# Shared pairs' halves by VectorE, other granules for masks, loads back and norms, and another order of the ring's slots

## Time and profile before

| | before |
|---|---|
| median of three runs | 2344.86 us |
| the profiled execution's own time | 2346.39 us |
| its span, first to last instruction | 2344.4 us |
| TensorE busy | 2286.9 us, 98% |
| VectorE, ScalarE, GpSimd busy | 1303.6, 748.2, 957.5 us |
| mean granted TensorE clock | 0.991 |
| DMA queues' share | 78% |
| landing of a plain weight (512 KB) | 4.4 us median |
| landing of a mixed weight (256 KB) | 3.2 us (ring), 3.6 us (extra slots) median |

### The profile page before, as it was taken

The page is one execution under the profiler, slowest core; times in us unless marked ns, Lnnn a source line. Parts: engine busy times, 40 slices in busy tenths (PEclk is TensorE's granted clock), DMA queues, the critical chain, the costliest instruction groups (busy, mean ns, idle before and its releaser), DMA issues.

```text
span 2344.4 us, 27397 instructions
## 1 busy us (share of the span) xinstructions
PE 2286.9 (98%) x10264; PEld 1891.1 (81%) x10264; DVE 1303.6 (56%) x1696; ACT 748.2 (32%) x1173; POOL 957.5 (41%) x686
## 2 busy tenths in 40 slices
PE   8999999999999999999999999898999999999899
PEld 7888787788888888888888888786788888877777
DVE  4332666857344448738235448687823545858660
ACT  3233554233343335202124326413113433632210
POOL 5455555587354522142034450516204544053610
PEclk9999999999999999999999999999999999999999
DMA  7799999878888878886678886666667887666755
GB/s 266 269 393 375 350 344 333 326 273 304 298 291 272 278 293 289 303 333 234 233 246 269 281 291 226 209 207 243 243 219 260 282 272 281 227 218 205 270 186 179
DMA packets 229158, 637.07 MB, mean 272 GB/s; under 512 B 23712, under 2 KB 32928, under 8 KB 225952
## 3 DMA queue, kind: packets, MB, share of 16 engines
q1 hardware_dynamic: 229024, 635.30, 78.0%
HBM read 483.10 MB, written 152.11 MB: 271 GB/s over the span
## 4 chain that ended last, share of the span: by engine, by line
PE 80%; DVE 10%; DMA 5%; issue 2%; SPq 1%; ACT 1%; POOL 1%; DVEq 0%; ACTq 0%
PE bank L1333 26%; PE bank L1335 26%; PE bank L1334 26%; PE bank L1353 1%; DVE acc L1627 1%; DMA mixed_w<-mixes 1%; DMA prod<-spilled_u 1%; DMA split_w<-w 1%; DVE prod L1908 1%; DMA w_more<-mixed_w 1%; DVE w L1973 1%; SPq L779 1%; DVE below L1806 1%; POOL w L1066 1%; DVE largest L1809 1%
## 5 line engine op out<-in xcount | busy, mean ns | idle before, releaser
L1066 POOL TENSOR_TENSOR w<-raw,w 128x512 fp32r<-128x512 f32 (+1 forms) x196 | 281.3, 1442 | 207.7 <-ACT w L1112 207.4
L1333 PE MATMUL bank<-w,prod_t 128*128 128x512 f32 x672 | 271.5, 404 | 10.5 <-DVE prod_t L2042 10.5
L1071 POOL TENSOR_TENSOR w<-w 128x512 fp32r<-128x512 f32 x138 | 196.2, 1446 | 207.6 <-ACT w L1287 207.3
L1335 PE MATMUL bank<-w,prod_t 128*128 128x512 f32 x672 | 264.7, 394 | 0.0
L1334 PE MATMUL bank<-w,prod_t 128*128 128x512 f32 x672 | 263.8, 393 | 0.0
L1333 PE MATMUL bank<-w,tok 128*128 128x512 f32 (+1 forms) x664 | 253.5, 382 | 3.9 <-POOL w L1066 3.0
L1335 PE MATMUL bank<-w,tok 128*128 128x512 f32 (+1 forms) x664 | 252.5, 380 | 0.0
L1334 PE MATMUL bank<-w,tok 128*128 128x512 f32 (+1 forms) x664 | 252.4, 380 | 0.0
L1333 PE MATMUL bank<-tok,w 128*128 128x512 f32 x640 | 249.0, 389 | 0.0
L1334 PE MATMUL bank<-tok,w 128*128 128x512 f32 x640 | 249.0, 389 | 0.0
L1335 PE MATMUL bank<-tok,w 128*128 128x512 f32 x640 | 249.0, 389 | 0.0
(11 more groups left out here) (219 smaller groups left out, 4681.4 us busy)
## 6 DMA issues: line engine op xcount, KB each, us to landing
w<-split_w SPq DMA_DIRECT2D x448, 512.0 KB, 4.4
split_w<-w SPq DMA_DIRECT2D x184, 512.0 KB, 6.2
w<-mixed_w SPq DMA_DIRECT2D x184, 256.0 KB, 3.2
w_more<-split_w SPq DMA_DIRECT2D x88, 512.0 KB, 5.2
w_more<-mixed_w SPq DMA_DIRECT2D x120, 256.0 KB, 3.6
rows<-x_dram SPq DMA_DIRECT2D x32, 512.0 KB, 5.3
mixed_w<-own SPq DMA_DIRECT2D x12, 1024.0 KB, 5.2
spilled_u<-prod SPq DMA_DIRECT2D x12, 1024.0 KB, 8.2
```

What stands on the lines that cost most here:

```text
L1066: pool.tensor_tensor(lo, words, hi, ALU.subtract).then_inc(lo_ready, 1)
L1071: pool.tensor_tensor(slot_of(g)[:, 1, :], slot_of(g)[:, 1, :].bitcast(F32), slot_of(g)[:, 0, :], ALU.subtract).then_inc(pool_lo, 1)
L1333: pe.matmul(out, left[0], right[0], start=first, stop=False)
L1335: return pe.matmul(out, left[1], right[0], start=False, stop=last)
```

## The change

- Pairs 5 and 6: VectorE lowers A12 (behind each k's sums) and A22 in `make_units`, and S1, S2, S4 in a new function `lower_sums`, right behind it. GpSimd keeps A11 and S3 (`lower_early`), with a semaphore of its own, and lowers T4's weights too, which VectorE did.
- In pairs 5 and 6 the extra slots take granules 4 to 7 of ten instead of 6 to 9.
- Wide blocks: the scratch of the picks lies over unit slots 2 to 4 (A12's and A22's words). Tiles 0 and 1 are picked at granules 175 and 177, tiles 2 and 3 at 209 and 210, and the choice is at 212 (before: 209, 211, 213, 215 and 218). ScalarE's cut of an odd hidden step waits for the picks that lie before it. The first two groups are masked at 213 and 214 (219, 220), and GpSimd multiplies their six chunks at 215 to 220 (221 to 226).
- Wide blocks: loads back of groups 0 to 3 at the last granules of products 2 to 5 of pair 6: 235, 239, 243, 247 (before 239, 251, 253, 255). Masks of groups 0 to 3 at 251, 253, 255, 257 (251, 255, 258, 261). Norms at 261, 264, 267, 270 (258, 261, 264, 267), the next block's first tokens at 275 and 277 (272, 273), their loads at 270 and 273 (266, 267).
- Block 0: ScalarE's counts three and four granules after VectorE's step instead of one and two. The own sets ten granules apart from 42 on (nine, from 44), mixed seven granules after the first load instead of five; the norm's constants at 164 instead of 158.

```diff
                     self.late_hi_at[odd + 9] = n
-                    self.units_lo_at.update({begun + 5: (n, "early"), odd + 8: (n, "A12"), odd + 10: (n, "A22"),
-                                             odd + 12: (n, "S1"), odd + 15: (n, "S2"), odd + 19: (n, "S4")})
+                    self.lower_at[odd + 2] = n
+                    self.units_lo_at[begun + 5] = n
...
         self.search_at = {m: k for k, m in enumerate(steps_at[1:COUNTS + 1])}
-        self.pick_from = self.start[("hidden", 2)] + 1 if wide else steps_at[COUNTS + 1]
-        self.search_end = self.pick_from + (2 if wide else 3) * TILES + 1
-        self.pick_at = {self.pick_from + (2 if wide else 3) * t: t for t in range(TILES)}
+        self.pick_from = steps_at[COUNTS + 1]
+        self.search_end = self.pick_from + 3 * TILES + 1
+        self.pick_at = {self.pick_from + 3 * t: t for t in range(TILES)}
+        if wide:
+            self.pick_from, begun = (self.start[("hidden", i)] + 3 - i for i in (1, 2))
+            self.pick_at = {self.pick_from + 1: 0, self.pick_from + 3: 1, begun: 2, begun + 1: 3}
+            self.search_end = begun + 3
         if wide:
-            self.back_at = {end["fast", SHARED_PAIRS[1], 3]: [0], shared_end: [1], out0 + 1: [2], out0 + 3: [3]}
-            read = {("up", c): out0 + at - 1 for c, at in enumerate((-1, 3, 6, 9))}
+            self.back_at = {end["fast", SHARED_PAIRS[1], q]: [c] for c, q in enumerate((2, 3, 4, 5))}
+            read = {("up", c): out0 + at - 1 for c, at in enumerate((-1, 1, 3, 5))}
...
                         for i, g in enumerate(GROUPS[:-1])}
-        self.mask_at[out0 + 9 if wide else out0 + 5 if later else out0 + 3] = GROUPS[-1]
+        self.mask_at[out0 + 5 if later else out0 + 3] = GROUPS[-1]
...
             self.read_hidden_at, self.hidden_at = {}, {}
-        self.norm_at = [out0 + 6 + (3 if later else 5) * t for t in range(TILES)]
-        self.tokens_at = [out0 + 20, out0 + 21] if later else [out1 + 2, out1 + 4]
+        self.norm_at = [out0 + (9 if wide else 6) + (3 if later else 5) * t for t in range(TILES)]
+        self.tokens_at = [out1 + 1, out1 + 3] if wide else [out0 + 20, out0 + 21] if later else [out1 + 2, out1 + 4]
         self.residual_load = [ups + 2, ups + 3, self.norm_at[0] + 3, self.norm_at[1] + 3]
-        self.tokens_load = [out0 + 14, out0 + 15] if later else [self.norm_at[2] + 3, self.norm_at[3] + 3]
+        self.tokens_load = [out0 + 18, out0 + 21] if wide else [out0 + 14, out0 + 15] if later else [self.norm_at[2] + 3, self.norm_at[3] + 3]
...
 SQUARE_LAG = 2
-COUNT_LAG = 1
+COUNT_LAG = [3, 1, 1, 1]
...
         _from, PHASE[_b, _phase[0]] = _m, _m
-        _order = [(_next + i) % RING for i in range(RING)] + list(range(RING, RING + EXTRA))
+        _order = [(_next + i) % RING for i in range(RING)]
+        _place = HALF if _phase[0] in SHARED_PAIRS else RING
+        _order[_place:_place] = range(RING, RING + EXTRA)
...
 OWN_SETS = range(FIRST_MIXES, FIRST_MIXES + 3 * HALF)
-OWN_FROM = {n: 44 + 9 * i for i, n in enumerate(OWN_SETS)}
+OWN_FROM = {n: 42 + 10 * i for i, n in enumerate(OWN_SETS)}
 OWN_LOADS = {at + i: (n, i) for n, at in OWN_FROM.items() for i in range(4)}
-OWN_AT = {at + 5: n for n, at in OWN_FROM.items()}
-OWN_STORES = {at + 6: n for n, at in OWN_FROM.items()}
-FIRST_NORM_LOAD = 158
+OWN_AT = {at + 7: n for n, at in OWN_FROM.items()}
+OWN_STORES = {at + 8: n for n, at in OWN_FROM.items()}
+FIRST_NORM_LOAD = 164
...
     _, p, q = granule.key
-    return products(p)[q] == VECTOR_LO and (p < SPILLED[0] or p in SHARED_PAIRS)
+    return products(p)[q] == VECTOR_LO and p < SPILLED[0]
...
-    return len(UNIT_LOS) * shared_round(b, n) + UNIT_LOS.index(what) + 1
+    names = EARLY_LOS if what in EARLY_LOS else UNIT_LOS
+    return len(names) * shared_round(b, n) + names.index(what) + 1
...
         below = sb("below", [P, GK, P], F32)
+        below_of = [over("below_wide", [P, GK, P], F32, u_at + 2 * HALF * 2 * P * 4) if wide else below for wide in WIDE]
+        assert GK * P <= 3 * HALF * 2 * P
...
-            def lower_units(b, n, what):
...
+            def lower_early(b, n):
...
                     if m in plan.units_lo_at:
-                        lower_units(b, *plan.units_lo_at[m])
+                        lower_early(b, plan.units_lo_at[m])
...
                         act.wait_ge(spilled[c], 16 * b)
+                if odd:
+                    act.wait_ge(search, b * SEARCHES + PICKED + 2 * (2 + 2 * n))
...
                 s4 = unit_sums[:, SUM_SLOT["S4"][1], :, :]
-                dve.wait_ge(units_lo, unit_lo(b, n, "S3"))
+                hi, lo = UNIT_SLOT["A12"]
+                dve.wait_ge(early_lo, unit_lo(b, n, "S3"))
                     dve.tensor_tensor(s4[:, k, :], a12[:, k, :], s3[:, k, :], ALU.subtract).then_inc(unit_summed, 1)
+                    dve.wait_ge(operand_hi, highs(b, "hidden", (2 * n + 1) * TILES + k + 1))
+                    dve.wait_ge(unit_summed, at * UNIT_SUMS + 1 + 2 * k + 2)
+                    dve.tensor_tensor(unit_r[:, lo, k, :], a12[:, k, :], unit_r[:, hi, k, :],
+                                      ALU.subtract).then_inc(units_lo, 1)
                 dve.tensor_tensor(unit_raw[:, 7, :, :], unit_raw[:, 7, :, :], a22, ALU.add).then_inc(unit_summed, 1)
+                dve.wait_ge(unit_summed, (at + 1) * UNIT_SUMS)
+                hi, lo = UNIT_SLOT["A22"]
+                dve.tensor_tensor(unit_r[:, lo, :, :], a22, unit_r[:, hi, :, :], ALU.subtract).then_inc(units_lo, 1)
+            def lower_sums(b, n):
+                at = shared_round(b, n) * UNIT_HIS
+                for name, done in (("S1", 4), ("S2", 2), ("S4", 3)):
+                    words, parts = (unit_raw, unit_r) if name in UNIT_SLOT else (unit_sums, unit_sums_r)
+                    hi, lo = UNIT_SLOT[name] if name in UNIT_SLOT else SUM_SLOT[name]
+                    dve.wait_ge(unit_sum_hi, at + done)
+                    dve.tensor_tensor(parts[:, lo, :, :], words[:, lo, :, :], parts[:, hi, :, :],
+                                      ALU.subtract).then_inc(units_lo, 1)
...
                 dve.wait_ge(search, at)
-                dve.scalar_tensor_tensor(out=below[:, :, :], in0=mag[:, :, t, :], scalar=tried[:, 0, t:t + 1],
+                dve.scalar_tensor_tensor(out=below_of[b][:, :, :], in0=mag[:, :, t, :], scalar=tried[:, 0, t:t + 1],
                 dve.wait_ge(search, at + 1)
-                dve.max(largest[:, t, :], below[:, :, :].rearrange("p k n -> p (k n)")).then_inc(search, 1)
+                dve.max(largest[:, t, :], below_of[b][:, :, :].rearrange("p k n -> p (k n)")).then_inc(search, 1)
...
```

More of the change, by code:

```diff
@@ L169, in __init__ @@
         self.units_at, self.early_sum_at, self.units_hi_at, self.early_hi_at = {}, {}, {}, {}
+        self.lower_at = {}
         self.late_hi_at, self.units_lo_at, self.units_cut_at = {}, {}, {}
@@ L488 @@
 UNIT_HIS = 4
-UNIT_LOS = ["A11", "S3", *(("A12", k) for k in range(HALF)), "A22", "S1", "S2", "S4"]
+UNIT_LOS = [*(("A12", k) for k in range(HALF)), "A22", "S1", "S2", "S4"]
+EARLY_LOS = ["A11", "S3"]
 def shared_round(b, n):
@@ L677, in program @@
         units_lo = sem("units_lo")
+        early_lo = sem("early_lo")
         shared_loaded = sem("shared_loaded")
@@ L1003, in sum_lo @@
                                    ALU.subtract).then_inc(sums_lo, 1)
-            def lower_units(b, n, what):
+            def lower_early(b, n):
                 at = shared_round(b, n)
[L1008 to L1015, removed]
-                    pool.tensor_tensor(unit_sums_r[:, lo, :, :], unit_sums[:, EARLY_RAW, :, :], unit_sums_r[:, hi, :, :],
-                                       ALU.subtract).then_inc(units_lo, 1)
-                elif what == "A12":
-                    hi, lo = UNIT_SLOT[what]
-                    for k in range(HALF):
-                        pool.wait_ge(unit_summed, at * UNIT_SUMS + 1 + 2 * k + 2)
-                        pool.wait_ge(operand_hi, highs(b, "hidden", (2 * n + 1) * TILES + k + 1))
-                        pool.tensor_tensor(unit_r[:, lo, k, :], unit_raw[:, lo, k, :], unit_r[:, hi, k, :],
-                                           ALU.subtract).then_inc(units_lo, 1)
-                elif what in UNIT_SLOT:
-                    hi, lo = UNIT_SLOT[what]
-                    pool.wait_ge(unit_summed, (at + 1) * UNIT_SUMS)
-                    if what == "S1":
-                        pool.wait_ge(unit_sum_hi, at * UNIT_HIS + 4)
-                    else:
-                        pool.wait_ge(operand_hi, highs(b, "hidden", (2 * n + 2) * TILES))
-                    pool.tensor_tensor(unit_r[:, lo, :, :], unit_raw[:, lo, :, :], unit_r[:, hi, :, :],
-                                       ALU.subtract).then_inc(units_lo, 1)
-                else:
-                    hi, lo = SUM_SLOT[what]
-                    pool.wait_ge(unit_sum_hi, at * UNIT_HIS + {"S2": 2, "S4": 3}[what])
```

(20 more changed lines are left out.)

## The result

The median of four runs is 2320.85 us (2318.17 to 2323.42); the kernel before, run beside it, has 2345.01. The ratio is 0.9898 (95% interval 0.9881 to 0.9915): 24.2 us faster, where 40.1 were forecast. 2304.8 was named and 2288 to 2319 as the range; the time lies 2 us above it, next to rival (b) in size. The profiled execution took 2320.16, with a span of 2317.9: 26.5 less than before.

The account below looks back on a forecast made before the run. TensorE, busy 98%, bounds the kernel; its stalls within reach are 66.9 us. Blocks 2 and 3 give 33.7, block 0 6.4, together 40.1: 2306.3 from the profiled 2346.39, 2304.8 for the median; range 2288 to 2319.

Parts of the forecast that it names:

- rival (b): Pair 5: VectorE's queue no shorter, 7.9 us stays; out 0 keeps 8.8, block 0 gives 3; 2319 us, chance 0.14.
- Ring order: Pair 5: T3's loads go out behind the last B11 load, at 1483.0; T3 is lowered by 1493.4, in time.
- Picks: Ahead of pair 5: tiles 0 and 1 picked by 1491.5, when the hidden banks' cut begins, 2.0 us sooner than before.
- Pair 5 and its price of 2.2: Lowerings of VectorE and GpSimd that meet take 2.2 us; 3.0 us of 7.9 lost stays, bounds 1 and 7.
- Pair 6: T3 is lowered when product 1 wants it, so the 4.2 us stall goes; 0.6 us of 11.5 stays (0 to 3).
- its 0.7: Pair 6: the cut of the hidden banks follows T3's last copy, 0.7 us behind the pair's start.
- Out 0: Masks ahead of turned halves move the stall to k 2, 4, 6 (3.9, 1.8, 2.5 us); 8.3 of 8.8 stays.
- Block 0: Later counts save about 1.9 us, the own mix at 89 about 4, the last but one keeps 3; 6.4 of 9.4 go.
- (a): Masks run at 0.69 us, lowerings cost 1.7 a pair; out 0 and pair 5 keep 1 each; 2286 us, chance 0.17.
- (c): Mid-pair lock: VectorE's twelve sums and lowerings last 1.43 us each, delaying product 4's bank; slower, 2363 us, chance 0.03.

Follow-up runs that it names:

- The two single runs: Kernel before with only block 0's own-set and norm-load edits: 2337.50 us, ratio 0.9947; with only ScalarE's later counts there: 2341.13 us, ratio 0.9973.
- the last experiment: Changed kernel with earlier extra-slot loads and spread out 0 masks, plus ScalarE's copies of S2, S4, S1 behind T4's: 2317.08 us, ratio 0.9874.

## Why the forecast was wrong, step by step

**The step that failed is "Ring order".** It says that T3's loads "go out behind the last B11 load, when granule 177 is used". The table gives the extra slots as their last reader granule `_g - 1`, the last one of the hidden step (179), whatever their place in the ring: a line beside the diff, unchanged by it. The loads went out 5.4 us later, at the pair's start, in all four pairs. The waiting copies hold ScalarE's cut, and the cut holds the chain. With that condition at 177 the time was 2304.1, near the 2304.8 on record. That it is so near is luck, as other steps' errors cancel in it: the four pairs still lost 12.0 us then where the sum has 7.2, and block 0 gave 4.5 more than reckoned.

**Picks.** They end at 1481.8, 3.1 us behind the pair's start, as reckoned; but T3's copies end later, so the new wait cost nothing. With the early loads both end together: the picks at 1481.3, the cut from 1481.37.

**Pair 5 and its price of 2.2.** Right: 2.26 measured, and 3.7 lost with the early loads against 3.0. The sum for the pair was nearly right once its cut came when I said.

**Pair 6.** The stall at product 1 went, and its 0.7 failed for the same reason as pair 5; the early loads show that 2.2 would stay and not 0.6, as T3's last copy ended 7.2 us behind the first issue and not 5.5, the loads going out beside B11's. The picks, the masks ahead of the pair and the loads back were not run by themselves; that they took the stall away is read from the trace (no wait of TensorE there, and no mask of groups 1 to 3 waits for a load back).

**Out 0.** The 3.9 at k 2 is exact. The stalls at k 4 and 6 were forecast at 1.8 and 2.5 and measured at 0 and 0.7. A part is my sum: with turn 4's half at 1647.7, TensorE wants turn 6's after 24 x 0.2268 + 2 x 0.48 = 6.4, at 1654.1 and not 1653.0, which makes 1.4 and not 2.5. For the rest, the second group's masks ended 6.5 us behind turn 2's half (1623.8 to 1630.3) where I had 7.3, since the first of each group goes at 0.75 and I had put all four at 1.65. And behind the first stall TensorE had a granted clock of 0.63 from 1624.0 to 1628.4, so that k 2's twelve matmuls took 4.4 us instead of 2.7, and k 4 was wanted that much later; this reading is from the timeline alone, no run tested it. 6.7 stayed of 8.3.

**Block 0.** Under-sized: 10.9 against 6.4. The three stalls that I name, 1.9, about 4 and some 5, add up to 10.9 and not to the 9.4 that the sum takes them from, and I let 3 us of the last-but-one mix's stay, while none stayed. The two single runs show that the mechanisms overlap: either edit alone removes that stall and the one behind the mix at 85, and behind the stall that I gave to ScalarE's count stood a second one, which only the own sets remove.

**The rivals.** (b) came nearest in time, by another mechanism than its own: pair 5 kept 7.0 of 7.9 because its cut was late. (a) did not come: lowerings cost 2.26 and masks 1.75. (c) did not come in the changed kernel, but its price of 1.43 and its deciding point, product 4's bank, are what the last experiment ran into.

## What to carry to other kernels

When a buffer is given earlier work, look up what its load waits for in the code, not only its place in the order; an old condition beside the diff can hold it. An engine's idle stretch next to a critical chain may be what keeps that chain fast: putting T4's lowering into GpSimd's idle 9.8 us cost 24 us. And where an engine is 96% loaded in a stretch, moving a collision within that stretch moves the wait, it does not remove it.

## What the runs showed of the hardware

Four mixed loads of 256 KB that were issued in pair 5 with nothing else under way (from 1478.86) landed 2.5 to 4.3 us after their issue, median 3.1. Issued two granules earlier, between plain loads (from 1473.43), they took 5.2 to 5.9, median 5.4; in pair 6, likewise between plain loads, 3.8 to 5.1, median 4.8.

Operations on SBUF words by VectorE and GpSimd that meet repeatedly pace each other. Three sizes agree with the sum of both durations less 0.25 to 0.3 us: 128x256 with 128x512 0.42 + 1.29, measured 1.43 to 1.47; masks 0.75 + 1.29, measured 1.75; lowerings 1.22 + 1.29, measured 2.26. VectorE's operations with one input in PSUM (0.61 an add, squares 0.69) left GpSimd at 1.3 and were not lengthened. The Trainium skill, "SBUF — State Buffer", § Who interferes with whom, says both: a VectorE instruction with two inputs in SBUF contends with a GpSimd one that reads SBUF, and one with at most one such input, outside the two-port modes, does not. These traces agree with that. The section also calls the shared pair of ports an exclusive lock; if each waited for the whole of the other's instruction, a meeting would cost 0.25 to 0.3 us more than these runs show.
